# Closing the last Block without GpSimd's drain, and the last expert tile's down weights split into the gate and up buffers

## The reference

```python
x = x + attn(_layernorm(x))                  # mixer and dense feed-forward, not touched by the change
xn = _layernorm(x)
router_logits = einsum('bsh,he->bse', xn, Wr)                # H=512, E=8
probs = softmax(router_logits, axis=-1)
topk_w, topk_idx = top_k(probs, 2)
topk_w = topk_w / sum(topk_w, axis=-1, keepdims=True)
combine = einsum('bsk,bske->bse', topk_w, one_hot(topk_idx, E))
g = einsum('bsh,ehi->besi', xn, Wg)                          # I=352
u = einsum('bsh,ehi->besi', xn, Wu)
h = silu(g) * u
y = einsum('besi,eih->besh', h, Wd)
out = x + einsum('bse,besh->bsh', combine, y)
```

## Time and profile before

| | us |
|---|---|
| median of 3 runs (1465.37 to 1467.95) | 1465.78 |
| the profiled execution's time | 1464.82 |
| its span, first to last instruction | 1463.1 |
| PE busy in the span | 1391.6 (95%) |
| DVE busy | 964.7 (66%) |
| ACT busy | 642.4 (44%) |
| POOL busy | 436.9 (30%) |

### The profile page before, as it was taken

The page is one execution under the profiler, slowest core; times in us unless marked ns, Lnnn a source line. Parts: engine busy times, 40 slices in busy tenths (PEclk is TensorE's granted clock), DMA queues, the critical chain, the costliest instruction groups (busy, mean ns, idle before and its releaser), DMA issues.

```text
span 1463.1 us, 21007 instructions
## 1 busy us (share of the span) xinstructions
PE 1391.6 (95%) x7360; PEld 1116.0 (76%) x7360; DVE 964.7 (66%) x1337; ACT 642.4 (44%) x1123; POOL 436.9 (30%) x457
## 2 busy tenths in 40 slices
PE   6899999999999997999999999999998899999995
PEld 4677777756666665888888888888886789999994
DVE  6879697789999995332333323333356889999994
ACT  4544444555555554212122112121112278888883
POOL 2512121347767775011010101011001134334332
PEclk9999999999999999999999999999999999999997
DMA  9133122822222223310000000030046623443422
GB/s 202 60 115 111 62 87 85 253 110 102 102 101 102 108 102 109 122 29 29 15 29 14 29 28 29 14 108 0 19 147 237 233 57 68 80 78 70 76 43 37
DMA packets 84362, 124.49 MB, mean 85 GB/s; under 512 B 27695, under 2 KB 44079, under 8 KB 84272
## 3 DMA queue, kind: packets, MB, share of 16 engines
q1 hardware_dynamic: 71488, 103.62, 21.7%
q0 software_dynamic: 8736, 18.62, 7.3%
q10 hardware_dynamic: 4048, 1.10, 0.3%
HBM read 81.37 MB, written 43.78 MB: 86 GB/s over the span
## 4 chain that ended last, share of the span: by engine, by line
PE 57%; DVE 1%; DMA 1%; issue 1%; ACT 0%; POOL 0%; ACTq 0%; DVEq 0%; POOLq 0%
PE fin_bank L1905 52%; PE fin_bank L2036 1%; PE fin_bank L2015 1%; PE fin_bank L2055 1%; DMA out_dram<-result_rows,put_idx 1%; PE fin_bank L2028 0%; PE fin_bank L1973 0%; PE fin_bank L1961 0%; PE fin_bank L2081 0%; DVE ff_w_lo L1679 0%; DVE fi_bn L1714 0%; ACT ff_w_hi L1561 0%; DVE gu_lo L1809 0%; POOL out_dram L1515 0%; PE fin_bank L1971 0%
## 5 line engine op out<-in xcount | busy, mean ns | idle before, releaser
L1641 DVE TENSOR_TENSOR ff_prod<-ff_prod,fin_bank 128x512 f32<-128x512 f32 x64 | 44.0, 688 | 262.9 <-PE fin_bank L1905 262.9
L1905 PE MATMUL fin_bank<-ff_hT_hi,ff_w_hi 128*128 128x512 f32 x512 | 202.6, 396 | 3.2 <-DVE ff_w_lo L1649 3.2
L1905 PE MATMUL fin_bank<-ff_hT_lo,ff_w_hi 128*128 128x512 f32 x512 | 202.5, 395 | 0.0
L1905 PE MATMUL fin_bank<-ff_hT_hi,ff_w_lo 128*128 128x512 f32 x512 | 202.3, 395 | 0.0
L1441 POOL TENSOR_TENSOR ff_w_lo<-ff_stage,ff_w_hi 128x1024 fp32r<-128x1024 f32 (+1 forms) x24 | 56.5, 2356 | 410.3 <-ACT ff_w_hi L1551 406.0
L542 DVE SCALAR_TENSOR_TENSOR conv_acc<-raw,conv_w,conv_acc 128x512 f32<-128x512 f32 x144 | 115.8, 804 | 42.0 <-ACT raw L348 35.8
L647 PE MATMUL pj_bank<-hT_hi,w_in_hi 128*128 128x512 f32 x336 | 136.1, 405 | 7.3 <-POOL w_in_lo L295 4.4
L1536 ACT ACTIVATE ff_prod<-fin_bank 128x512 f32<-128x512 f32 x64 | 38.3, 598 | 231.5 <-PE fin_bank L1905 231.3
L647 PE MATMUL pj_bank<-hT_lo,w_in_hi 128*128 128x512 f32 x336 | 133.3, 397 | 0.0
L647 PE MATMUL pj_bank<-hT_hi,w_in_lo 128*128 128x512 f32 x336 | 132.4, 394 | 0.0
L1809 DVE TENSOR_TENSOR gu_lo<-wx,gu_hi 128x1408 fp32r<-128x1408 f32 x78 | 124.3, 1632 | 0.7 <-ACT gu_hi L1580 0.7
(11 more groups left out here) (306 smaller groups left out, 3201.9 us busy)
## 6 DMA issues: line engine op xcount, KB each, us to landing
cv_rows<-cst SPq DMA_DIRECT2D x12, 1024.0 KB, 4.3
cv<-cv_rows SPq DMA_DIRECT2D x16, 768.0 KB, 4.3
zs_rows<-zst SPq DMA_DIRECT2D x8, 1024.0 KB, 6.5
zs<-zs_rows SPq DMA_DIRECT2D x16, 512.0 KB, 5.3
wx<-in_L_ffn_Wg_dram SPq DMA_DIRECT2D x8, 704.0 KB, 8.5
wx<-in_L_ffn_Wu_dram SPq DMA_DIRECT2D x8, 704.0 KB, 8.3
w_raw<-in_L_attn_in_proj_w_dram SPq DMA_DIRECT2D x32, 128.0 KB, 3.5
x<-_attn_hidden_states_dram SPq DMA_DIRECT2D x16, 256.0 KB, 5.5
```

Of the source, the lines that this page charges most:

```text
L1641: eng.tensor_tensor(prod[c][:, :], prod[c][:, :], up_ps[c][:, :], ALU.mult).then_inc(s["prod"], 1)
L1905: mm = eng.matmul(ps, w[a], x[b], start=first and i == 0, stop=last and i == 2)
```

## The change

Two things are edited, both at the end of `finish`. The last Block is opened with `no_gpsimd_drain=True`: at its end GpSimd's DRAIN is left out; the other four engines still issue theirs, and all five still meet in the barrier. And for the last tile, 38, the down weights are split into the first 1536 columns of `gu_hi` and `gu_lo`, seen as flat rows, instead of `wd_hi` and `wd_lo`; their split waits for the up product of tile 38 (`eu_ps` at 39) in place of the down product of tile 37 (`y_ps` at 38), and is written one iteration earlier, behind `gate(38)` on ScalarE and behind `product(38)` on VectorE. `down(38)` reads them there.

```diff
+        gu_flat = [t[:, :, :].rearrange("p a n -> p (a n)")[:, 0:NC * D] for t in (gu_hi, gu_lo)]
+
+        def down_place(j):
+
+            return gu_flat if j == SORT_TILES - 1 else [wd_hi[:, :], wd_lo[:, :]]
+
-        block = ctx.enter_context(nc.Block())
+        block = ctx.enter_context(nc.Block(no_gpsimd_drain=True))
...
             def weights_high(kind, j):
-                done = {"gate": "eg_ps", "up": "eu_ps", "down": "y_ps"}[kind]
-                ge(eng, s[done], j)
-                eng.activation(high[kind], raw_part(own[j], kind), ACT.Copy).then_inc(s["ew_hi"], 1)
+                if kind == "down" and j == SORT_TILES - 1:
+                    eng.wait_ge(s["eu_ps"], SORT_TILES)
+                else:
+                    ge(eng, s[{"gate": "eg_ps", "up": "eu_ps", "down": "y_ps"}[kind]], j)
+                out = down_place(j)[0] if kind == "down" else high[kind]
+                eng.activation(out, raw_part(own[j], kind), ACT.Copy).then_inc(s["ew_hi"], 1)
...
             for j in range(SORT_TILES):
-                weights_high("down", j)
+                if j < SORT_TILES - 1:
+                    weights_high("down", j)
...
                 if j + 1 < SORT_TILES:
                     gate(j + 1)
+                if j == SORT_TILES - 2:
+                    weights_high("down", j + 1)
...
-                eng.tensor_tensor(low[kind], raw_part(own[j], kind), high[kind].bitcast(F32), ALU.subtract)\
-                   .then_inc(s["ew_lo"], 1)
+                hi, lo = down_place(j) if kind == "down" else (high[kind], low[kind])
+                eng.tensor_tensor(lo, raw_part(own[j], kind), hi.bitcast(F32), ALU.subtract).then_inc(s["ew_lo"], 1)
...
                 if j + 1 < SORT_TILES:
                     product(j + 1)
+                if j == SORT_TILES - 2:
+                    weights_low("down", j + 1)
...
-                    w = [t[0:n, c * D:(c + 1) * D] for t in (wd_hi, wd_lo)]
+                    w = [t[0:n, c * D:(c + 1) * D] for t in down_place(j)]
```

More of the change, by code:

```diff
@@ L1887, in _ @@
             for j in range(SORT_TILES):
-                weights_low("down", j)
+                if j < SORT_TILES - 1:
+                    weights_low("down", j)
                 if j + 3 < SORT_TILES:
```

## The result

The changed kernel takes 1457.70 us (median of 5 runs, 1457.26 to 1459.69) against 1465.37 for the kernel before (median of 5, 1464.36 to 1467.95): ratio 0.9948, interval 0.9936 to 0.9960. That is 7.7 us less (5.9 to 9.4 by the interval), where 7.51 were forecast.

What follows compares the result with a forecast made beforehand. The prediction took a tail of single steps after 1440.6 us, closed by GpSimd's drain, to set the end. It summed 6.44 + 1.07 = 7.51 us off the 1465.78 median to 1458.3 us, range 1456.0 to 1462.6.

Steps and rivals of the forecast that it cites:

- The drain, 6.44 us: Closing line of the last Block: GpSimd's DRAIN lies wholly on the path, so leaving it out saves 6.44 us.
- The bounds from the earlier Block ends: Drains of 384, 279 and 1902 ns at earlier Block ends; 0.3 us might come back, at most all 6.44.
- zero for what comes back: At the program's end: none of the drain's 6.44 us returns in another form.
- The second edit's mechanism: Last tile: weight split starts 0.13 us after the up product; scatter 37's landing becomes late next; end 1.07 us earlier.
- the landing of scatter 36: Tail: started 1439.86, took 4.53 us, lands 1444.39, just in time by 0.01 for scatter 37 to follow its result.
- The near tie: Scatter 36's landing at 1444.39 against scatter 37's result at 1444.40: each tenth the landing is later costs a tenth.
- 1447.9 or 1449.6: Tile 38's result ready time with the last down product at full or half clock, both before scatter 37's landing at 1449.77.
- no wait shows behind the span: Rival outside the program: the drain's wait moves behind the span, leaving only the second edit's 1.07, 1464.7; chance 0.14.
- nothing came back in the barrier: Case of rival "less than the sum": half the drain returns in the barrier, 3.2 us, 1461.5; the rival's chance 0.09.
- the last scatter does not follow its own result: Against rival "more than the sum": last scatter not held by the one before, 6.44 + 2.90, 1456.4; chance 0.03.
- slower: Rival outside the program: unretired software DMAs retired at end and next start, 12.88 less 7.51 saved, 1471.2; chance 0.04.

Runs made afterwards that it cites:

- the first edit's run: Kernel before with only GpSimd's drain left out of the last Block, down weights kept in wd_hi and wd_lo: 1459.41 us against 1466.12, ratio 0.9952.
- the second edit alone: Kernel before with only the last tile's down weights moved to gu_hi and gu_lo, GpSimd's drain kept: 1464.20 us against 1466.12, ratio 0.9988.
- the one behind scatter 18: Kernel before with two more GpSimd drains, behind scatter 18's issue and just ahead of the Block's own: 1463.30 us, one execution.
- those behind 10, 20 and 30: Changed kernel with the Block's drain kept and GpSimd drains added behind the issue of scatters 10, 20 and 30: 1458.82 us against 1465.91, ratio 0.9953.

## Why the prediction was right, point by point

**The drain, 6.44 us: right.** Alone it gave 6.7 by the medians (5.1 to 9.1 by the interval), and 6.5 at the closing line. The bounds from the earlier Block ends were read wrongly: their 279, 384 and 1902 ns are waits for GpSimd's own last instruction and not the price of a drain, and 6438 is so much more by the software DMAs, which those ends did not have. The forecast did not need the reason. The choice of zero for what comes back was right: 1.70 us around the span after, 1.72 before. A wait for what GpSimd has left undone does not show in this time: the 82 ns for each DMA are not paid anywhere in it. What lies outside the time is not recorded.

**The second edit's mechanism: right; its size: 0.32 us too high in the trace.** The split started 0.13 us behind the up product; the gap became 1.61 against 1.6; the scatter before became what is late. The edit gave 0.75 and not 1.07, and the step that failed is the landing of scatter 36: the sum put it just in time by 0.01, with 4.53 us of flight from the trace before. It took 4.76 after, so that the chain of landings begins one scatter earlier than I had it, and scatter 37 starts 4.66 us behind the mark (1445.11), where the sum had 4.42. The near tie was named as worth a tenth for each tenth, and these 0.24 us are that; the other 0.08 is scatter 37's own flight, 4.67 against 4.59. One execution was too little to price a flight: the last three scatters of the ten traces took 4.4 to 5.3 us. The tie was also misread by its own rows: a scatter starts 0.83 us behind a landing but 0.78 behind a result, so the landing at 1444.39 would have given 1445.22 and not 1445.18. The times give the edit 0.4 to 3.1 us, which does not decide between these sizes.

**The clock before was taken from one execution.** The sum compares with a tail whose clock fell in the middle of the last down product. In the first edit's run it fell ahead of it, and there the second edit is worth 1.7 us. The 1.9 between the medians of the second edit alone and of the kernel before lies near that, but of each timed run only the mean granted clock over the whole span is recorded, which does not place the fall in the tail, so its share in the median is not shown. The forecast that with the edit the half clock is covered ("1447.9 or 1449.6", before a landing at 1449.77) held in the second edit's own trace: 1449.55 before 1450.19.

**Sum: 7.51 forecast, 7.67 measured, and 8.1 when timed again.** That it fits to 0.2 us is in part luck: the interval goes from 5.9 to 9.4, the two edits timed alone add up to 8.6 (6.7 and 1.9), and the spans of the two profiled executions differ by 7.1, of which 0.3 lies ahead of the tail. The rivals: no wait shows behind the span; nothing came back in the barrier; the last scatter does not follow its own result while the one before is in flight, as the run without scatter 37 shows; and with nothing coming back, slower had no mechanism here.

## What to carry to other kernels

A program's end is a stage of its own: read the closing line of each Block, where drains stand that no busy time counts, and count what each of them waits for. A drain of GpSimd cost 82 ns here for each software DMA since the last one. It can be left out where semaphores already prove the landings, or be paid mostly in advance where GpSimd is idle; look at the scatters behind such a drain, since the one behind scatter 18 put them into a chain of landings and those behind 10, 20 and 30 did not. And where two paths arrive together at the end, follow the second one to its own source before pricing an edit on the first, with durations from more than one execution: here it was a chain of three landings.

## What the runs showed of the hardware

- A drain of GpSimd took 46 ns right behind another drain, and, with everything landed, 945 with 11 software DMAs since the last drain, 2907 with 35 and 6438 with 78: 46 ns and 82 for each, all of them of 128 rows of 512. Begun with a scatter still on its way, it ended 42 to 43 ns for each DMA behind the landing (with 43, 27, 20 and 20 of them).
- An accumulating scatter of 128 rows of 512 landed 4.4 to 5.3 us after its start among the last three of each kernel, and one that waited for a landing started 0.83 or 0.84 us after it.
- GpSimd took 1.55 us for a scatter with no split of VectorE beside it, 1.94 to 1.97 with a split running for its first 0.4 to 0.5 us, and 2.5 to 3.0 with splits beside it from end to end; with a split that began 0.5 us after it, 1.59.
- After a gap of 1.6 us TensorE's clock was still granted in full through the last down product in two executions (the changed kernel, and the one without scatter 37) and was at half for all or most of it in four others, one of them of the same changed kernel; after 3.70 us it fell in the middle of the product once and before it twice. With 14 matmuls in the gap it stayed at full in the one execution seen.
